# First four tiles of the last matrix product normalised and turned in f32 before their scale is known, and the weight turned by DMA

## The reference

```python
x = x + attention(_layernorm(x), ctx, Wq, Wkv_expand, Wout)   # causal cross attention, 16 heads of 64
x = x + _L0_ffn_ref(_layernorm(x), L0_ffn_weight)

def _L0_ffn_ref(x, weight):
    w_fp8, w_scale = _quant_e4m3(weight)      # scale = max|w| / 448, values rounded to e4m3
    x_fp8, x_scale = _quant_e4m3(x2d)         # scale = max|x| / 448 over ALL rows
    return ((x_fp8 @ w_fp8.T) * (x_scale * w_scale)).astype(bfloat16)
```

## Time and profile before

| | us |
|---|---|
| median of 3 runs | 1737.17 |
| lowest and highest | 1736.21, 1738.05 |
| the profiled execution | 1736.76 |
| its span in the profile | 1734.8 |
| PE busy | 1706.3 |
| DVE busy | 1337.4 |
| ACT busy | 672.6 |
| POOL busy | 182.7 |

### The profile page before, as it was taken

The page is one execution under the profiler, slowest core; times in us unless marked ns, Lnnn a source line. Parts: engine busy times, 40 slices in busy tenths (PEclk is TensorE's granted clock), DMA queues, the critical chain, the costliest instruction groups (busy, mean ns, idle before and its releaser), DMA issues.

```text
span 1734.8 us, 27825 instructions
## 1 busy us (share of the span) xinstructions
PE 1706.3 (98%) x11485; PEld 810.6 (47%) x11513; DVE 1337.4 (77%) x1910; ACT 672.6 (39%) x638; POOL 182.7 (11%) x142
## 2 busy tenths in 40 slices
PE   7999999999999999999999999999999999999998
PEld 4544444445444544454445444544454444544444
DVE  8976687788866887788778877787778665877786
ACT  6632242223322332233223322332233222799985
POOL 0000000000000000000000000000000002255565
PEclk9999999999999999999999999999999999999999
DMA  9346645553545554545454545545554443799997
GB/s 351 105 112 161 152 97 119 136 147 87 128 121 134 109 125 114 139 107 126 121 128 122 114 130 131 112 104 125 133 125 111 97 86 71 264 314 323 324 250 217
DMA packets 387977, 258.95 MB, mean 149 GB/s; under 512 B 341920, under 2 KB 344480, under 8 KB 387616
## 3 DMA queue, kind: packets, MB, share of 16 engines
q1 hardware_dynamic: 387872, 257.47, 56.2%
HBM read 113.25 MB, written 67.11 MB: 104 GB/s over the span
## 4 chain that ended last, share of the span: by engine, by line
PE 84%; DVE 11%; ACT 3%; issue 1%; DMA 1%; SPq 0%; DVEq 0%; ACTq 0%
PE ps_all L730 34%; PE ps_all L746 32%; PE ps_all L903 12%; DVE m_buf L1271 3%; PE ps_all L713 3%; PE ps_all L683 1%; DVE n_buf L1265 1%; PE ps_all L755 1%; DVE tile_space L1340 1%; DVE hsum L1334 1%; DVE tile_space L1282 1%; DVE tile_space L1328 1%; PE ps_all L832 1%; DVE hmax L1323 1%; ACT n_buf L989 1%
## 5 line engine op out<-in xcount | busy, mean ns | idle before, releaser
L730 PE MATMUL ps_all<-m_buf,tile_space 128*128 128x504 f16 x3072 | 667.7, 376 | 0.6 <-DVE m_buf L1271 0.3
L746 PE MATMUL ps_all<-n_buf,tile_space 128*128 128x512 f16 x3024 | 667.4, 379 | 0.6 <-DMA tile_space<-tile_space 0.6
L730 PEld LDWEIGHTS ps_all<-m_buf,tile_space 128*128 128x128 f16 x3072 | 297.8, 98 | 351.9 <-issue 6.7
L746 PEld LDWEIGHTS ps_all<-n_buf,tile_space 128*128 128x128 f16 x3024 | 293.1, 98 | 356.6 <-issue 7.0
L575 POOL TENSOR_TENSOR rstd_x<-veps_x,minus_half 128x1 f32<-128x1 f32 x64 | 35.3, 551 | 1399.6 <-DVE veps_x L1295 1399.6
L1015 ACT ACTIVATE tile_space<-tile_space,neg_mean 128x1024 f32<-128x1024 f32 x56 | 64.3, 1149 | 278.1 <-DVE neg_mean L1360 278.1
L1011 ACT ACTIVATE tile_space<-tile_space,score_scale 128x1024 f32<-128x1024 f32 x64 | 73.4, 1147 | 233.2 <-DVE tile_space L1328 232.2
L1007 ACT ACTIVATE tile_space<-tile_space 128x1024 f16<-128x1024 f32 x64 | 67.6, 1057 | 190.5 <-DVE tile_space L1340 190.5
L1282 DVE SCALAR_TENSOR_TENSOR tile_space<-tile_space 128x1024 f16<-128x1024 f32 x64 | 78.4, 1225 | 70.7 <-ACT tile_space L1007 70.7
L1334 DVE TENSOR_REDUCE hsum<-tile_space 128x16 f32<-128x1024 f32 x64 | 77.9, 1217 | 58.3 <-ACT tile_space L1011 58.3
L1277 DVE SCALAR_TENSOR_TENSOR tile_space<-tile_space 128x1024 f16<-128x1024 f32 x64 | 78.3, 1223 | 52.8 <-ACT tile_space L1001 52.8
(11 more groups left out here) (170 smaller groups left out, 1566.9 us busy)
## 6 DMA issues: line engine op xcount, KB each, us to landing
tile_space<-in_x_dram SPq DMA_DIRECT2D x128, 512.0 KB, 4.0
x_scratch<-tile_space SPq DMA_DIRECT2D x56, 512.0 KB, 3.1
m_buf<-x_scratch SPq DMA_DIRECT2D x32, 512.0 KB, 5.6
out_dram<-m_buf SPq DMA_DIRECT2D x32, 512.0 KB, 4.3
tile_space<-x_scratch SPq DMA_DIRECT2D x24, 512.0 KB, 5.9
out_dram<-tile_space SPq DMA_DIRECT2D x24, 512.0 KB, 4.7
m_buf<-in_L_xattn_Wq_dram SPq DMA_DIRECT2D x4, 1024.0 KB, 11.9
n_buf<-in_L_xattn_Wout_dram SPq DMA_DIRECT2D x4, 1024.0 KB, 13.1
```

The lines of the kernel that those rows point to most:

```text
L730: mm = nc.tensor.matmul(ps_s[:, half * HALF:half * HALF + RH], left[:, ls, c * P:(c + 1) * P], m_buf[:, rs, c, half * RH:(half + 1) * RH], ...
L746: mm = nc.tensor.matmul(to[:, cols], left[:, ls, j * P:(j + 1) * P], right[:, rs, j, cols], start=(c == 0 and i == 0), stop=(c == CT - 1 a ...
```

## The change

It has these parts.

1. `turn_w8` and `copy_w8` are gone. SP turns the eight blocks of the weight by DMA, two in each of the steps 57 to 60, behind `turn_p`. The layout of `w8_t` differs: the product reads four blocks of 128 columns that lie 1024 elements apart (`w8_at`).
2. Tiles 0 to 3 are normalised before the scale is known: ACT writes `y_rows` in f32 as soon as their rows are back, PE turns them in f32 (`turn_y`), ACT copies tiles 0 and 2 to SBUF. Once the scale is there, they are rounded in turned form, with one number per tensor in place of one per row (`small[:, 7:8]`, `small[:, 9:10]`), into the buffers that PE reads. Tiles 0 and 1 are rounded by halves. Both operands of these passes of DVE lie in SBUF (`entry_u_t` and `v_t` or `a_t`), where those of lines 1632 and 1637 have one in PSUM.
3. The numbers per row for the other tiles are made by POOL, behind the scale.
4. The first product starts on half of its input (`first_linear`). There are 4 unread matmuls in the gap, and none behind it.
5. Tiles 4 to 9 keep their natural order: the even one of a pair is rounded first and turned by PE, the odd one second, by DMA (`first_pair`). From tile 10 on the order is that of before. The values of tiles 4, 6 and 8 are made by DVE. ACT's list is written out for the first tiles.

```diff
+                if known and t >= T - TB:
+                    for a in W8_AT.get(tt, ()):
+                        sp.wait_ge(w8_ready, CT)
...
+                        sp.dma_start_transpose(w8_t[:, a, :].rearrange("p (c r) -> p c r", r=P),
+                                               w8_raw[:, a, :]).then_inc(w8_turned, 16)
...
-            turn_rows(3)
...
+            pool.wait_ge(quant_ready, 1)
+            pool.wait_ge(kept, 2 * T - 1)
+            nc.gpsimd.tensor_tensor(quant_a[:], rstd1[:], small[:, 7:8].to_broadcast([P, T]), ALU.mult).then_inc(rows_quant, 1)
+            pool.wait_ge(rows_quant, 3)
+            nc.gpsimd.tensor_tensor(quant_b[:], mean1[:], quant_a[:], ALU.mult).then_inc(rows_quant, 1)
...
+            nc.gpsimd.tensor_scalar(quant_a20, quant_a[:], ROUND_UNDER, None, ALU.mult).then_inc(rows_quant, 1)
...
+            def w8_at(c, half):
+                return w8_t[:, 4 * half:4 * half + 4, c * P:(c + 1) * P]
...
+            def first_linear():
+                for c in range(CT):
+                    if c % 4 == 0:
+                        pe.wait_ge(r_ready, c // 4 + 1)
+                    for half in range(2):
+                        mm = nc.tensor.matmul(y_at(0, half), rt_t[0][:, c * P:(c + 1) * P], w8_at(c, half),
+                                              start=(c == 0), stop=(c == CT - 1))
+                mm.then_inc(y_full, 1)
...
+            pe.wait_ge(end_step, 4)
+            turn_y(0)
+            turn_y(1)
             pe.wait_ge(x_amax_rows, 1)
             nc.tensor.transpose(ps_o[:, 0:P], spread, ident[:]).then_inc(x_amax_turned, 1)
...
-            run_on(GAP_MATMULS, ps_all[:, 3 * HALF:4 * HALF])
+            turn_y(2)
+            pe.wait_ge(y_copied, 2)
+            turn_y(3)
             pe.wait_ge(x1_ready, T + 1)
-            turn_r(1, 0, 0, True)
-            run_on(TURN_MATMULS, ps_all[:, 0:HALF])
...
+            for k in range(GAP_MATMULS):
+                nc.tensor.matmul(ps_all[:, 3 * HALF:4 * HALF], ident_bf[:], w8_raw[:, k, 0:HALF], start=True, stop=True)
+            pe.wait_ge(w8_turned, 16 * CT)
+            first_linear()
+            linear(1, 1, rt_t[1])
...
+            for n, t in enumerate(Y_ORDER):
+                act.wait_ge(got_x1[t], 16)
+                nc.scalar.activation(y_rows[n], x2[t], ACT.Identity, bias=y_bias[:, t:t + 1],
+                                     scale=rstd1[:, t:t + 1]).then_inc(y_made, 1)
...
+            entry_magnitudes(0)
+            for k in range(1, 4):
+                entry_magnitudes(k)
+                entry_values(k)
+            entry_magnitudes(4)
             act.wait_ge(quant_ready, 2)
...
+            scaled(0, 0, True)
+            entry_magnitudes(5)
+            entry_values(5)
+            scaled(1, 1, True)
+            magnitudes(4, 4)
+            magnitudes(5, 5)
+            scaled(2, 0)
+            values(5, 5)
+            magnitudes(6, 6)
+            scaled(3, 1)
+            magnitudes(7, 7)
+            values(7, 7)
+            magnitudes(8, 8)
+            scaled(4, 0)
+            magnitudes(9, 9)
+            values(9, 9)
...
+            for k, (t, cols) in enumerate(ENTRY):
+                if k in ENTRY_BY_DVE:
+                    dve.wait_ge(y_copied, t // 2 + 1)
+                    then(nc.vector.tensor_scalar(v_t[t % 2][:, cols], entry_y[t][:, cols], small[:, 7:8], None, ALU.mult))
+                else:
+                    dve.wait_ge(v_ready, k if k < 4 else k - 1)
+                dve.wait_ge(u_ready, k + 1)
+                nc.vector.scalar_tensor_tensor(out=a_t[t % 2][:, cols], in0=entry_u_t[t % 2][:, cols], scalar=ROUND_LEAST,
+                                               in1=v_t[t % 2][:, cols], op0=ALU.max, op1=ALU.add).then_inc(a_done, 1)
+                dve.wait_ge(a_done, k + 1)
+                if t == 2:
+                    dve.wait_ge(y_full, 1)
+                nc.vector.scalar_tensor_tensor(out=entry_to[t][:, cols], in0=entry_u_t[t % 2][:, cols], scalar=ROUND_LEAST,
+                                               in1=a_t[t % 2][:, cols], op0=ALU.max, op1=ALU.subtract).then_inc(r_ready, 1)
...
+            def first_pair(k):
+                n = 2 * k + 2
+                if n in VALUES_BY_DVE:
+                    values(n)
+                shifted(n, 0)
+                if k >= 3:
+                    dve.wait_ge(r_full, k - 2)
+                rounded(n, 0, r_t[k % 2])
+                if k == 1:
+                    copy_rt(k + 1, k % 2)
+                shifted(n + 1, 1)
+                if k > 1:
+                    copy_rt(k + 1, k % 2)
+                rounded(n + 1, 1, rows_buf[:, (k + 1) % 4])
```

More of the change, by code:

```diff
@@ L317, in tile_of @@
         def tile_of(n, parity):
[L318 removed]
+            return n if isinstance(n, int) and n < NATURAL else n + 1 if parity == 0 else n - 1
         y_ps = [ps_all[:, 0:H], ps_all[:, HALF:HALF + H]]
@@ L809, in step @@
                     scores(xt_buf[1 - e], between, m_chunk)
-                if last and 1 <= tt <= W8_EARLY:
-                    turn_w8(tt - 1)
                 if b == 2 and is_step(tt, 5):
@@ L883, in _, with turn_r, y_at @@
                 batch(pe, b, step, unroll=(b == B - 1))
-            for a in range(W8_EARLY, CT):
-                turn_w8(a)
-            def turn_r(count, m, buf, first=False):
+            def turn_r(count, m, buf):
                 pe.wait_ge(r_ready, count)
-                if not first:
+                if not is_step(m, 0):
                     pe.wait_ge(rt_ready, m)
                 turn(r_ps, r_t[buf], r_full, ident_bf)
+            def w8_at(c, half):
+                return w8_t[:, 4 * half:4 * half + 4, c * P:(c + 1) * P]
+            def y_at(e, half):
+                return y_ps[e][:, half * HALF:(half + 1) * HALF].rearrange("p (a r) -> p a r", r=P)
+            def first_linear():
[6 more added lines that the diff above has]
+                mm.then_inc(y_full, 1)
             def linear(t, e, left, between=None):
@@ L918, in linear_pair @@
                 else:
-                    pe.wait_ge(rt_ready, k + 2)
+                    if known and k == 1:
+                        pe.wait_ge(r_ready, 5)
+                    else:
+                        pe.wait_ge(rt_ready, k - 1)
                     linear(t, 0, rt_t[(i + 1) % 2])
-                pe.wait_ge(rows_turned[i], q * 16 + 16 if i else q * 16)
+                if known and k == 1:
+                    pe.wait_ge(r_ready, 6)
+                else:
+                    pe.wait_ge(rows_turned[i], q * 16 + 16 if i > 1 else q * 16)
@@ L922, in linear_pair, with turn_y @@
                 linear(t + 1, 1, turned_buf[:, i],
-                       None if known and k + 1 >= BY_DMA else lambda: turn_r(t + 4, k + 2, i % 2))
+                       None if known and k + 1 >= BY_DMA else
+                       lambda: turn_r((t + 2 if known and t + 3 < NATURAL else t + 3) + BEHIND_ENTRY, k - 1, i % 2))
+            def turn_y(n):
+                pe.wait_ge(y_made, n + 1)
+                turn(Y_PS[n], y_rows[n], y_turned)
+            pe.wait_ge(end_step, 4)
+            turn_y(0)
@@ L944, in _ @@
+            pe.wait_ge(w8_turned, 16 * CT)
+            first_linear()
+            linear(1, 1, rt_t[1])
+            for k in range(1, 8):
+                linear_pair(k // 4, k % 4)
+            with pe.Fori(2, (BY_DMA - 1) // 4) as q:
                 for i in range(4):
@@ L1068, in step @@
                     grow_m(1)
-                if last and 1 <= tt <= W8_EARLY:
-                    copy_w8(tt - 1)
                 if is_step(tt, TB - 1) and not last:
@@ L1621, in first_values, with shifted @@
                                         ALU.add).then_inc(v_first, 1)
-            def shifted(t, e, first=False):
-                dve.wait_ge(u_ready, t + 1)
-                if first:
-                    dve.wait_ge(v_first, 1)
-                elif late_odd(t):
-                    dve.wait_ge(v_first, 2 + (t - 2 * BY_DMA) // 2)
+            def shifted(n, e):
+                known = isinstance(n, int)
+                dve.wait_ge(u_ready, n + BEHIND_ENTRY)
+                if known and n in VALUES_BY_DVE:
+                    dve.wait_ge(v_first, VALUES_BY_DVE.index(n) + 1)
+                elif late_odd(n):
+                    dve.wait_ge(v_first, len(VALUES_BY_DVE) + 1 + (n - 2 * BY_DMA) // 2)
+                elif known:
+                    dve.wait_ge(v_ready, ENTRY_VALUES + sum(m not in VALUES_BY_DVE and not late_odd(m) for m in range(ENTRY_TILES, n + 1)))
                 else:
-                    dve.wait_ge(v_ready, t - (t - 2 * BY_DMA) // 2 if isinstance(t, int) and t >= 2 * BY_DMA else t)
+                    dve.wait_ge(v_ready, ENTRY_VALUES + n - ENTRY_TILES + 1 - len(VALUES_BY_DVE))
                 nc.vector.scalar_tensor_tensor(out=a_t[e], in0=u_ps[e], scalar=ROUND_LEAST, in1=v_t[e], op0=ALU.max,
@@ L1659, in quantise_pair @@
             def quantise_pair(q, i):
                 k = q * 4 + i
```

(14 more changed lines are left out.)

168 lines of the change are left out of this document (85 added, 83 removed).

## The result

The changed kernel takes 1738.74 us (median of 20 runs, 1737.85 to 1740.68), the kernel before 1736.37 us (20 runs, 1735.31 to 1738.27).

What follows compares the result with a forecast made beforehand. PE, busy 98%, bounds the kernel, with DVE and ACT on the chain before the linear stage. Savings of -5.6 shrink to -1.9 by waits and become +2.9 by the port: 1736.76 + 2.9 = 1739.7 us, range 1734.5 to 1741.7.

Steps and rivals of the forecast that it cites:

- Part 1: Last batch of the attention: PE's two turns of the weight leave the chain, -0.9 us; broken-up product input costs nothing.
- Part 2: Start of the linear stage: first matmul at 1490.96 instead of 1495.64, -4.7 us including 0.9 from the weight's turns.
- rival (4): Start of the linear stage: PE not free at 1490.96, turning tile 3 late; 0.5 us at most, no chance given.
- Part 3: Stream of the linear stage: PE turns 22 tiles instead of 25, two fewer in the stream, -0.9 us.
- Part 4: Tiles 0 to 9: DVE's list and the DMA turn lose 2.0 us by tile 5, then 4.2 by tile 9.
- the weave: Tiles 5 to 9: PE waits for scaled behind DVE's copy and rounding; 18.9 us, not 14.7, so 4.2 lost.
- Rival (2): Tiles 5 to 9: ACT's list costs less than added up; without the 4.2 us loss, -6.1 us; chance 0.10.
- Part 5: Tiles 2 and 3: POOL's additions hold DVE's passes over two SBUF operands, +2.0 us twice under two-sided holding.
- B: Tiles 2 and 3: DVE and POOL hold each other out; +2.9 us in sum, tile 9 at 1534.3; chance 0.50.
- C: Tiles 2 and 3: POOL doesn't wait for DVE, its second addition holds nothing; +0.7 us in sum; chance 0.13.
- A: Tiles 2 and 3: DVE's two-input passes aren't held; -1.9 us in sum, -1.3 when only values(4) is; chance 0.20.
- Rival (3): Gap or PE's new waits near tiles 2 to 5: PE's clock falls to half; up to +6 us; chance 0.07.

Runs made afterwards that it cites:

- the fifth experiment: The kernel before with the weight turned by DMA alone, PE's six turns in the gap replaced by unread matmuls; 1734.95 us, ratio 0.9994.
- e1: The changed kernel with POOL's first addition waiting until DVE has rounded tile 3; 1734.89 us, ratio 0.9994 to the kernel before.
- e2: The changed kernel with the magnitudes of tiles 2 and 3 in PSUM; 1735.98 us, ratio 0.9998 to the kernel before.
- e8: The changed kernel with scaled(4) and scaled(5) moved ahead of magnitudes(8) and magnitudes(9) in ACT's list; 1736.83 us, ratio 1.0000 to the kernel before.

## Why the prediction was right

**Part 1** was forecast at -0.9 and measured 0.97 (the fifth experiment), with the matmuls' pace untouched.

**Part 2**, the start, was forecast at 1490.96, with the start's clock as in the old execution. The measured 1490.18 plus those 0.85 is 1491.03, by the chain that was written down. PE was free in time, so rival (4) falls: its wait of 0.78 at L932 is for DVE.

**Part 3** was forecast at -0.9: from the first matmul to tile 9 PE turns three tiles where it turned five, 0.45 each.

**Part 4**, the weave, was forecast at 18.9 from tile 5 to tile 9, and 0.6 for the clashes of values(6) and values(8). Without a clock fall it measures 19.4 to 19.6, and 15.3 with the odd tile first. Rival (2), that the loss doesn't arise, falls. In the second pair the mechanism is the forecast's, and so is its length: 9.45 forecast, 9.54 to 9.56 measured, with PE waiting for scaled(7) (2.02 in the changed kernel; in e1 0.82 for scaled(6) and 1.03 for scaled(7)). In the first pair (9.86 and 10.09 in e1 and e2) the wait lies elsewhere than forecast: not before the second half of tile 6, for scaled(5), but mainly before the second half of tile 5, for scaled(4) (1.71; in e1 and e2 1.72, with only 0.37 left for scaled(5)). scaled(4) stands behind magnitudes(8), which waits 2.73 for rounded(6) (the rows at 1515.69 and 1516.83), and rounded(6) is late because values(6) was held by the addition of 1510.33. By the lengths in the rows, without that hold PE would have waited for scaled(5), as forecast, and tile 7 would have started 9.45 behind tile 5; so the hold moves the wait and adds 0.4 to 0.6 (9.86 and 10.09), close to the forecast's 0.6. That is an estimate: no run has the natural order without the hold. The sum of part 4 is right, the place of its first wait is not. What the forecast did not see at all is that in this pair the loss goes when two `scaled` are moved up in ACT's list (e8).

**Part 5**, the port, was the step that decided between faster and slower, and it is B. The holds were forecast at 2.0 and 2.0; they measure 1.81 and 1.92, and they fall on rounded(2) and shifted(3), not on shifted(2) and shifted(3): shifted(2) had begun 0.33 before the addition and kept it out. The order was off by a third of a microsecond, the sum was not, since with two-sided holding it matters little which pass meets the addition. C is excluded by POOL's 2.88, 2.55 and 3.15, A by DVE's 3.03 and 3.15. DVE's list is 3.75 later by the two (e1), where 4.0 were forecast, and 0.2 for POOL's five short operations: these took 0.32 to 0.70 us and not 0.24 to 0.3, and yet DVE's eight half passes ended in the 5.5 us that were forecast without them. At tile 5 the removal of the holds gave 3.0 to 3.2: F+20.25 and F+20.51, not F+19.74, because each experiment brought a wait of its own. With them tile 5 is at F+23.48, not at F+23.94, so this step of the sum was 0.5 too large.

The rule of the Trainium skill (SBUF — State Buffer, the section on the two separate sides) has a VectorE operation with two SBUF inputs and a GpSimd operation that reads SBUF shut each other out for the whole instruction, whoever is first. The trace agrees, to 0.15 us at the end. The same section, under "Who interferes with whom", names `tensor_scalar` in its two-port modes as a second kind that contends, and the trace agrees here too: 2.60 and 1.46 in place of 0.81.

**Rival (3)**, the clock, had 0.07. The fall came once, at 1518 and not in the gap. It followed stretches in which PE had little to do (0.89 us of work between 1512 and 1514, 0.29 between 1516 and 1518), and cost about 1.2 us (20.74 against 19.42 to 19.64) of the 1.7 of PE's work; the forecast had it hidden wholly in B. The agreement at tile 9 is closer than the terms: 1534.40 was measured for tile 9 and 1534.3 forecast, but with the clock of the start taken out the forecast is 1533.5, and the terms are -0.4 at tile 5, +0.1 between 5 and 9, +1.2 for the clock. The agreement to 0.1 us is luck; the sum is right within 1 us. In the new gap PE had f32 turns, four unread matmuls and idle stretches of 1.77 and 0.78 us, and the granted clock stayed at 1.00 in all windows from 1484 to 1518. So the fall did not come there that the prediction took for likely by the Trainium skill (TensorE: Matmul & The Clock Gate, part 4).

What stays open: why the clock falls near 1518 in one execution of the changed kernel and in none of the profiled ones of its relatives, and how often it does. Its share in the median is not known; the changed kernel's fastest runs are 2.5 us above the fastest of before (1737.85 against 1735.31), so the 2.4 us of the medians hardly hang on it.

In short: the change brought 4.6 us before the first product and 0.9 in turns, and gave back 9.2 between the first product and tile 9, because DVE no longer had a lead: 3.2 to the exclusion at tiles 2 and 3, 4.2 to the weave together with the hold of values(6), 0.6 that stays with the odd tile first too (15.3 against PE's own 14.7), 1.2 to the clock in the execution shown. That is 3.7 more, and 2.8 with the 0.85 of the start. Without the clash and the weave the same change is worth 5 to 6 us: 1730.94 against 1736.10 and 1730.40 against 1736.67, timed side by side.

## What to carry to other kernels

When a stage is started earlier, look at who loses the lead: the engine that had worked ahead in the old gap now sets the pace, and costs that were hidden behind its lead (an operation put late in an in-order list, a clash for a port) come to the surface one by one. When an experiment moves an operation, ask in which stretch it can act, and read the gain there: here a total of 2.0 us was all of one pair's loss and nothing of the next one's, not half of both. Before two engines stream over SBUF at the same time, look at where each input lies: one operand in PSUM was enough to let DVE's passes run beside POOL's additions. And where they must clash, arrange that the pass on the critical path asks first; the other then waits, and costs nothing.
